# All activation groups transposed by VectorE into SBUF, their low parts taken by GpSimd, down products one group later

## The reference, cut to what matters

```python
x = x + conv(x, K) * mask              # state-space kernel K (512 taps), one per row of 32
x = x + einsum('bct,bcd->bdt', x, W1[cond])
x = x + einsum('bct,bcd->bdt', x, W2[cond])
gate = x @ Wg.T + 0.5 * (x @ Ag[i].T) @ Bg[i].T      # i: the sample's LoRA index
up   = x @ Wu.T + 0.5 * (x @ Au[i].T) @ Bu[i].T
act  = silu(gate) * up                               # 1376 hidden columns
x = x + act @ Wd.T + 0.5 * (act @ Ad[i].T) @ Bd[i].T
```

## Time and profile before

| | |
|---|---|
| median of 3 runs | 1037.53 us (1036.66 to 1037.77) |
| the profiled execution | 1037.1 us, its span 1035.3 us |
| granted TensorE clock | 0.995 mean |
| PE busy | 1003.2 us (97%), weight loads 883.2 us (85%) |
| DVE busy | 762.7 us (74%) |
| ACT busy | 421.2 us (41%) |
| POOL busy | 486.4 us (47%) |
| DMA | 135.5 MB, mean 131 GB/s |

### The profile page before, as it was taken

How to read it: one execution, slowest core, us unless ns; L and a number is a source line. 1 busy time by engine, 2 the same in 40 slices (tenths; PEclk the granted TensorE clock), 3 DMA queues, 4 the chain that set the end, 5 groups by cost and what they waited for, 6 DMA issues and landing times.

```text
span 1035.3 us, 19774 instructions
## 1 busy us (share of the span) xinstructions
PE 1003.2 (97%) x5668; PEld 883.2 (85%) x5668; DVE 762.7 (74%) x2087; ACT 421.2 (41%) x660; POOL 486.4 (47%) x301
## 2 busy tenths in 40 slices
PE   2998989999999999999999999999999999999998
PEld 2665778889889988988889899988989899899987
DVE  8333367788778877777788778877777787788774
ACT  7003144444434444444444434444344444434431
POOL 0703455554444544555554454544555554444541
PEclk9999989999999999999999999999999999999999
DMA  9899343433433333424333333334253433333320
GB/s 333 254 393 336 127 142 99 128 115 105 115 106 113 99 116 101 143 77 141 102 117 115 103 111 100 112 103 135 82 145 93 124 114 106 112 109 103 111 74 21
DMA packets 101125, 135.50 MB, mean 131 GB/s; under 512 B 26411, under 2 KB 59692, under 8 KB 101100
## 3 DMA queue, kind: packets, MB, share of 16 engines
q1 hardware_dynamic: 100524, 135.12, 42.3%
q10 hardware_dynamic: 576, 0.08, 0.0%
HBM read 118.11 MB, written 16.99 MB: 130 GB/s over the span
## 4 chain that ended last, share of the span: by engine, by line
PE 93%; DMA 3%; DVE 3%; SPq 1%; issue 1%; ACT 0%; DVEq 0%
PE ps L1028 47%; PE ps L1060 27%; PE ps L1038 8%; PE ps L1006 5%; DMA tr<-kpad 2%; PE ps L1049 1%; PE ps L1083 1%; PE ps L1019 1%; PE ps L1016 1%; PE ps L1082 1%; PE ps L1017 1%; DMA x1p<-yo 1%; SPq L212 0%; DVE xs L731 0%; PE ps L980 0%
## 5 line engine op out<-in xcount | busy, mean ns | idle before, releaser
L480 POOL TENSOR_TENSOR bst<-braw,bst 128x1024 fp32r<-128x1024 f32 (+1 forms) x96 | 212.7, 2215 | 323.5 <-ACT bst L587 323.5
L839 DVE STREAM_TRANSPOSE ps<-act_t 32x128 f32<-32x128 f32 x1008 | 325.4, 323 | 14.9
L1028 PE MATMUL ps<-wg_hi,x_hi 128*128 128x512 f32 (+2 forms) x768 | 293.7, 382 | 0.2 <-issue 0.2
L1028 PE MATMUL ps<-wg_lo,x_hi 128*128 128x512 f32 (+2 forms) x768 | 290.8, 379 | 0.0
L1028 PE MATMUL ps<-wg_hi,x_lo 128*128 128x512 f32 (+2 forms) x768 | 290.6, 378 | 0.0
L609 ACT ACTIVATE at_hi<-ps 128x512 fp32r<-128x512 f32 (+1 forms) x95 | 53.4, 562 | 334.4 <-DVE ps L839 275.7
L839 DVE STREAM_TRANSPOSE ps<-x3m 32x128 f32<-32x128 f32 x496 | 160.1, 323 | 10.0 <-ACT x3m L554 1.4
L1028 PEld LDWEIGHTS ps<-wg_hi,x_lo 128*128 128x128 f32 x768 | 144.7, 188 | 25.2
L1028 PEld LDWEIGHTS ps<-wg_hi,x_hi 128*128 128x128 f32 x768 | 145.0, 189 | 23.1 <-issue 0.4
L1028 PEld LDWEIGHTS ps<-wg_lo,x_hi 128*128 128x128 f32 x768 | 145.0, 189 | 22.7
L1060 PE MATMUL ps<-wd_lo,at_hi 128*128 128x288 f32 x696 | 148.9, 296 | 0.0
(11 more groups left out here) (157 smaller groups left out, 1108.8 us busy)
## 6 DMA issues: line engine op xcount, KB each, us to landing
braw<-in_tb SPq DMA_DIRECT2D x256, 128.0 KB, 2.7
braw<-in_tb SPq DMA_DIRECT2D x128, 96.0 KB, 2.4
adraw<-in_tad SPq DMA_DIRECT2D x128, 88.0 KB, 1.9
tr<-kpad SPq DMA_DIRECT2D x16, 512.0 KB, 7.0
x1p<-yo SPq DMA_DIRECT2D x16, 512.0 KB, 5.7
xb<-in_x SPq DMA_DIRECT2D x32, 256.0 KB, 2.9
agraw<-in_ta SPq DMA_DIRECT2D x128, 64.0 KB, 1.8
bdraw<-in_tbd SPq DMA_DIRECT2D x128, 64.0 KB, 2.2
```

Of the source, the lines that this page charges most:

```text
L480: sub(v, b_from(p, q), v.bitcast(F32), ALU.subtract).then_inc(s["blo"], 1)
L839: last = V.transpose(to[cols].rearrange("f (k n) -> f k n", n=P)[:, :, rows], of[rows].rearrange("n (k f) -> n k f", f=P)[:, :, cols])
L1028: last = mm(bank[:, 0:n], x3s[a][:, k, :], wgs[b][:, k, o:o + n], start=(k == 0 and a + b == 0), stop=False, skip_group_check=True)
```

## The change

- All three groups are turned by DVE, out of `act_t` into a new SBUF buffer `a_raw`; the PE transposes of group 0 are gone (but one `a_turn` at the very end). Group 0's turn has 16 pieces of 32 x 96.
- `at_hi` and `at_lo` are made from `a_raw`; the low part is now POOL's (`a_low` in the POOL block).
- `silu` waits until the turn of the group before has left `act_t` (`atv`); the turn waits until POOL has read `a_raw` (`alo`).
- On PE, `down` of group 1 moves from the end of its tile behind `chunk(p, 1, 0)` of the next, `down` of group 2 behind `chunk(p, 1, 1)`, and `down` of group 0 to the end of its own tile; new waits on `mul` stand ahead of `chunk(p, 0, 0)` and `chunk(p, 2, 0)`.
- x is loaded, summed and split two tiles ahead; ACT, POOL and SP have another order; the store of a tile goes out one tile later.

```diff
+        a_raw = sb("a_raw", [P, T])
...
             def tile_io(t, p, here, there, mixes, first=False, second=False, last=False):
                 if not last:
                     load_ag(t + 1, there)
-                    load_ad(t + 1, there)
+                if mixes is not None:
+                    load_wbd(t + 1, mixes, p)
+                if not first:
+                    load_bd(t, here)
                 load_b(t, here, p, 2, t * 3 + 1)
+                if mixes is not None:
+                    load_x(t + 2)
                 if not last:
                     load_b(t + 1, there, 1 - p, 0, t * 3 + 2)
-                if mixes is not None:
-                    mix_data(t + 2, mixes, p)
-                if not first:
-                    store_out(t - 1)
+                    load_ad(t + 1, there)
+                if not first and not second:
+                    store_out(t - 2)
                 if not last:
                     load_b(t + 1, there, 1 - p, 1, t * 3 + 3)
-                    load_bd(t + 1, there)
...
+            def a_low(t, q):
+                n = PAIRS[q][1] - PAIRS[q][0]
+                pool.wait_ge(s["ahi"], t * 3 + q + 1)
+                sub(ats[1][:, 0:n * P], a_raw[:, 0:n * P], ats[0][:, 0:n * P].bitcast(F32), ALU.subtract
+                    ).then_inc(s["alo"], 1)
...
+            def tile_lows(t, p, first=False, ahead=True, last=False):
+                if not first:
+                    a_low(t - 1, 2)
                 b_low(t, p, 1)
+                if ahead:
+                    x_sum(t + 2)
+                b_low(t, p, 2)
+                a_low(t, 0)
                 if not last:
                     ag_low(t + 1)
-                b_low(t, p, 2)
+                    ad_low(t + 1, 1 - p)
+                if ahead:
+                    x1_low(t + 2)
+                a_low(t, 1)
                 bd_low(t)
                 if not last:
-                    ad_low(t + 1, 1 - p)
                     b_low(t + 1, 1 - p, 0)
...
+            def tile_act(t, p, first=False, ahead=True, last=False):
+                if not first:
+                    silu(t - 1, 1 - p, 2, t * 3 - 1)
+                    a_high(t - 1, 1)
                 t_high(t)
                 b_high(t, p, 1, None if first else t * 3)
-                silu(t, p, 0)
                 if not last:
                     ag_high(t + 1)
-                a_high(t, 0)
+                    x3_copy(t + 1)
+                if not first:
+                    a_high(t - 1, 2)
+                silu(t, p, 0, None if first else t * 3)
+                a_high(t, 0, None if first else t)
                 if not first:
                     td_high(t - 1)
                 b_high(t, p, 2, t * 3 + 1)
-                silu(t, p, 1)
+                if not last:
+                    b_high(t + 1, 1 - p, 0, t * 3 + 2)
+                silu(t, p, 1, t * 3 + 1)
                 bd_high(t, first)
                 if not last:
+                    x3_high(t + 1, t * 3 + 3)
+                if ahead:
+                    x1_high(t + 2)
+                if not last:
+                    ad_high(t + 1, 1 - p, None if first else t)
                     x3_keep(t + 1, 1 - p, None if first else t)
...
-            def a_turn(t, q):
+            def a_turn(t, q, free=None):
+                n = PAIRS[q][1] - PAIRS[q][0]
                 dve.wait_ge(s["mul"], t * 3 + q + 1)
-                turn(atp, act_t[:], GRID).then_inc(s["atv"], 1)
+                if free is not None:
+                    dve.wait_ge(s["alo"], free)
+                turn(a_raw[:, 0:n * P], act_t[:, 0:n * P], GRID).then_inc(s["atv"], 1)
...
             def tile_dve(t, p, first=False, second=False, last=False):
+                t_mask(t, p)
                 if not first:
                     act_mul(t - 1, 1 - p, 2)
-                    a_turn(t - 1, 2)
-                t_mask(t, p)
                 t_turn(t)
-                if not first:
-                    a_low(t - 1, 2)
                 t_low(t)
+                if not first:
+                    a_turn(t - 1, 2, t * 3 - 1)
                 if not last:
                     x3_turn(t + 1, GRID[0:8])
                 act_mul(t, p, 0)
+                a_turn(t, 0, None if first else t * 3)
+                if not first:
+                    td_mask(t - 1, 1 - p)
+                    td_turn(t - 1)
+                    td_low(t - 1)
                 if not last:
                     x3_turn(t + 1, GRID[8:16], True)
-                if not first:
-                    td_mask(t - 1, 1 - p)
-                    td_turn(t - 1)
-                a_low(t, 0)
-                if not first:
-                    td_low(t - 1)
+                act_mul(t, p, 1)
+                if not first:
                     out_sum(t - 1, 1 - p, None if second else (t - 1) * 16)
-                act_mul(t, p, 1)
-                a_turn(t, 1)
-                a_low(t, 1)
                 if not last:
                     x3_low(t + 1)
+                a_turn(t, 1, t * 3 + 1)
...
             def tile_pe(t, p, first=False, last=False):
+                if not first:
+                    pe.wait_ge(s["mul"], t * 3 - 1)
                 pe.wait_ge(s["x3lo"], t + 1)
...
                 chunk(p, 1, 0)
+                if not first:
+                    down(t - 1, 1 - p, 1)
                 pe.wait_ge(s["tlo2"], t + 1)
                 lora_b(t, p, 0)
+                chunk(p, 1, 1)
                 if not first:
                     down(t - 1, 1 - p, 2)
-                a_turn(t, 0)
-                chunk(p, 1, 1)
+                lora_b(t, p, 1)
+                pe.wait_ge(s["mul"], t * 3 + 1)
+                chunk(p, 2, 0)
                 if not first:
                     lora_b_down(t - 1, 1 - p)
-                lora_b(t, p, 1)
-                chunk(p, 2, 0)
+                chunk(p, 2, 1)
+                lora_b(t, p, 2)
...
                 pe.wait_ge(s["adlo"], t + 1)
                 down(t, p, 0)
-                chunk(p, 2, 1)
-                lora_b(t, p, 2)
-                if not last:
-                    down(t, p, 1)
```

More of the change, by code:

```diff
@@ L186, in cond_resid_kernel @@
             ag aghi aglo ad adhi adlo b0 b1 bhi blo bd bdhi bdlo
-            bfree la tm tmt thi2 tlo2 x3k gu silu mul att atv dn ahi alo td tdm tdt tdhi tdlo accd evac ost""".split() + [
+            bfree la tm tmt thi2 tlo2 x3k gu silu mul att atv dn ahi alo td tdm tdt tdhi tdlo accd evac aend ost""".split() + [
             f"wl{n}" for n in range(NW)] + [f"u{q}" for q in range(C // 2)]
@@ L366, in block_io @@
                 tile_io(i * 2, 0, here[0:GB], here[GB:], None if last else mixes[0:GB], first=first)
-                tile_io(i * 2 + 1, 1, here[GB:], there, None if last else mixes[GB:], last=last)
+                tile_io(i * 2 + 1, 1, here[GB:], there, None if last else mixes[GB:], second=first, last=last)
             sp.wait_ge(s["kout"], 32)
@@ L630, in _ @@
             x3_keep(0, 0)
-            def tile_act(t, p, first=False, last=False):
+            x1_high(1)
+            def tile_act(t, p, first=False, ahead=True, last=False):
                 if not first:
-                    silu(t - 1, 1 - p, 2)
+                    silu(t - 1, 1 - p, 2, t * 3 - 1)
+                    a_high(t - 1, 1)
+                t_high(t)
+                b_high(t, p, 1, None if first else t * 3)
                 if not last:
-                    x1_high(t + 1)
+                    ag_high(t + 1)
+                    x3_copy(t + 1)
                 if not first:
                     a_high(t - 1, 2)
-                t_high(t)
-                if not last:
-                    x3_copy(t + 1)
-                b_high(t, p, 1, None if first else t * 3)
-                silu(t, p, 0)
-                if not last:
-                    ag_high(t + 1)
-                a_high(t, 0)
+                silu(t, p, 0, None if first else t * 3)
+                a_high(t, 0, None if first else t)
                 if not first:
@@ L649, in tile_act @@
                 b_high(t, p, 2, t * 3 + 1)
-                silu(t, p, 1)
+                if not last:
+                    b_high(t + 1, 1 - p, 0, t * 3 + 2)
+                silu(t, p, 1, t * 3 + 1)
                 bd_high(t, first)
                 if not last:
-                    x3_keep(t + 1, 1 - p, None if first else t)
-                    ad_high(t + 1, 1 - p, None if first else t)
-                    b_high(t + 1, 1 - p, 0, t * 3 + 2)
-                a_high(t, 1)
-                if not last:
-                    x3_high(t + 1, t * 3 + 3)
+                    x3_high(t + 1, t * 3 + 3)
[3 more added lines that the diff above has]
+                    ad_high(t + 1, 1 - p, None if first else t)
+                    x3_keep(t + 1, 1 - p, None if first else t)
             tile_act(0, 0, first=True)
@@ L664, in _ @@
                 tile_act(i * 2 + 1, 1)
-            tile_act(NT - 2, 0)
-            tile_act(NT - 1, 1, last=True)
```

(20 more changed lines are left out.)

61 lines of the change are left out of this document (29 added, 32 removed).

## The result

The changed kernel took 1059.2 us (median of 4 runs, 1057.2 to 1061.7) against 1037.1 for the kernel before in the same session: a ratio of 1.021, 95% interval 1.018 to 1.023. So it is slower, clear of noise; whether by more than 2% the interval leaves open. The forecast was 1058. The total is right to 0.1%, but, as the experiments show, not every term in it is.

What follows compares the result with a forecast made beforehand. PE was taken to bound the kernel, busy 97% of the span. 1037.1 - 10.6 (transposes) + 23.3 (product wait) + 1.7 (first tile) + 3 (last tile) + 3 (second wait) = 1057.5, median 1058; range 1044 to 1078.

Steps and rivals of the forecast that it cites:

- Bound and gain: PE alone sets the pace; removing group 0's transposes, 0.33 us a tile, takes 10.6 us off PE.
- The turn: DVE's pieces into SBUF do not overlap when partitions change: 0.325 us a piece, 5.20 a turn, bounds 0.24 and 0.336.
- the faster rival: DVE's turn pieces overlap, 0.24 us each, so nothing waits in the steady part: near 1030 us, chance 0.15.
- The product wait: PE at `chunk(p, 1, 0)` waits for `act_mul` behind group 1's turn: 0.75 us a tile, +23.3 over 31 tiles.
- the walk: Step-by-step timing from the end of `lora_b` through `x3_high`, `x3_low`, sixteen pieces, `silu` and `act_mul`, ending at 524.14.
- The second wait: PE at `lora_b_down` waits for DVE's `td_low`, margin 0.4 us, with possible POOL meetings: +3 us, bounds 0 and +20.
- The third rival: DVE meets POOL in every second tile at 0.8 us or more: +12 to 20, so 1067 to 1075, chance 0.27.
- The SP queue: A tile's store, issued behind other issues and some 7.6 us of index loads, delays `out_sum` but is hidden: costed at nothing.
- The ends: New waits in the first tile cost +1.7 us (0 to 5), in the last tile +3 (1 to 5).
- The sum: All terms added to the earlier kernel's 1037.1 give 1057.5 us for a profiled-like execution, 1058 at the median.

Runs made afterwards that it cites:

- e_pitch: Changed kernel with each piece of group 1's turn made as two halves and group 2 turned by columns, longer by design: 1079.1 us, one run.
- e_index: Changed kernel with SP's index loads cut in two, part at the block's start and part between its two tiles: 1047.3 us, ratio 1.011.
- the split turn: `e_index` with the first 6 of the 16 pieces of group 1's turn issued ahead of `x3_low`: 1029.6 us, ratio 0.992.
- e_idx_split1: `e_index` with 1 piece of group 1's turn issued ahead of `x3_low`: 1040.6 us, ratio 1.003.

## Why the prediction was right, and where it was not

- **Bound and gain.** Right. PE set the pace, and an undisturbed tile is 27.93 against 28.29, 0.36 less: the 0.33 us of transposes, whole.
- **The turn.** Right in kind: into SBUF as into PSUM, pieces don't overlap where they change partitions; `e_pitch` shows it. 0.315 us each, 0.325 was taken; 0.24 would have been the faster rival.
- **The product wait.** The mechanism is right: it stands in `e_index` 31 times and goes with the split turn. The size was off: 0.48 us a tile alone, 14 us in 30 tiles, and not 0.75 and 23. Of the difference, 0.16 is the length of the pieces (16 x 0.010) and 0.10 the overlap of the first piece with `x3_low`, which the walk left out though it had the rule for it in hand. In the changed kernel itself it stood in every second tile only, 7 us in all, where the forecast had it 31 times.
- **The second wait.** Wrong. Three us were put on `td_low` at `lora_b_down`; it came once, with 0.2. (The third rival, built on it, took POOL to idle a third of the time; with 57% busy it idles more than that.)
- **The SP queue.** This is the step that failed, as it was put: "With PE at its new, slower pace this is hidden; I cost it at nothing." It cost 11.8 us, by `e_index`, 11 of them in the steady part, and 18 there if the product wait that it hid is left out of the count. The forecast had seen the 7.6 us pause and the store at the end of the issues, and worked out a margin of 0.2 us, but looked at the store alone. It did not walk the other loads past the pause, nor ask what stands behind each of them on POOL and ACT.
- **The ends.** The first tile cost 1.5 for 1.7. The last cost 5.2 for 3: the wait for the product was 2.1 for 1.5, and the slow matmuls behind it (1.5) had been reckoned in the first tile only.
- **The sum.** 23.3 + 3 + 0 was forecast for the steady waits, 26.3, and 25 was found: 14 for the product wait when it stands alone and 11 for the pause, or 7 and 18 as they stand in the changed kernel. That the 1058 came out right was luck: one term too large met one that was missing.

## What to carry to other kernels

When a change moves loads or their consumers, walk every load past the longest pause of the queue that issues it, and for each that comes late ask what stands behind its consumer in program order; a load that nobody needs yet is no danger, but the instruction that takes it in may be. Waits that share a cause and stand side by side can't be priced one at a time: take the cause away (here 12 us) before taking away the waits (here 0, 6 and 4). And an alternating tile length is a sign of a loop body of two tiles, so look at what it does once.

## What the runs showed of the hardware

- Whether DVE starts an instruction before the last one's end depends on partitions: 0.61 us behind `x3_low` where the next begins at its partitions, 0.72 where it does not; 0.16 and 0.20 for halves of 0.22 and 0.19. I had not expected that the reading side alone holds a piece.
- DVE and POOL do get in each other's way. `t_low` took 410 ns in the median before and 609 now: in 31 of 32 tiles it begins some 0.33 us before the end of POOL's `at_lo`, and `bdst` begins before its own end. POOL's `bdst` there takes 1473 ns instead of 1295. The two instructions of DVE in the changed kernel, least/median/most in ns:

```profile
L899 DVE TENSOR_TENSOR t_lo<-tr,t_hi x32: 425/609/617, 127.8 to 1022.8; 128x256 fp32r<-128x256 f32 x32
```
```profile
L919 DVE TENSOR_TENSOR td_lo<-tdr,td_hi x32: 291/293/1421, 174.2 to 1055.7; 128x128 fp32r<-128x128 f32 x32
```

One `td_low` took 1.42 us instead of 0.29. Timelines of DVE and of POOL there:

```profile
319.28 1.42 DVE L919 TENSOR_TENSOR td_lo<-tdr,td_hi 128x128 fp32r<-128x128 f32 x1 [0.38 <-ACT td_hi L637]
```
```profile
319.26 1.29 POOL L462 TENSOR_TENSOR x_raw<-x_raw,xb 128x512 f32<-128x512 f32 x1 [4.34 <-DMA xb<-in_x]
```

It began 0.02 us behind `x_sum` and ended 0.15 behind its end: `td_low` was held for all of the other. This is the meeting of the third rival, once in 32 tiles and not in every second, and the 0.2 us at `lora_b_down` are all that came of it. SBUF — State Buffer of the Trainium skill, under who interferes with whom, has it that a DVE instruction with two SBUF inputs contends with a GpSimd instruction that reads SBUF, and this trace agrees. How much is lost is another matter: `t_low` became 0.20 longer where 0.33 of `at_lo` were left.
- A wait costs PE more than the lateness. In `e_idx_split1` the product ended 5.29 us into the tile, 0.10 behind the 5.19 at which PE could have gone on. The chunk started at 5.34 and its second matmul 0.34 later instead of 0.23, and the tile was 28.21, 0.28 longer. Even a product that is just in time costs something: in one tile of the changed kernel it ended at 5.12, the chunk started at 5.20 and its second matmul 0.31 later, and the tile took 28.02 instead of 27.93.
